# First retention rows loaded in the order of their use, and split queries stacked with their gap in one transfer

## The reference, cut to what matters

```python
h = s4d_kernel(log_dt, inv_A_real, A_imag, B, C=x, L=512)      # (16, 192, 512)
h = h + retention(layernorm(h))                                # 8 heads, keys 64, values 128
h = h + top1_attention(layernorm(h))                           # 16 heads of 32

# retention, per batch of 192 tokens
q, k = rope(x @ Wq), rope(x @ Wk);  v, g = x @ Wv, x @ Wg
scores = (q * 64 ** -0.5) @ k.T * decay_mask
o = rmsnorm(scores @ v) * g_norm_weight * (g * sigmoid(g))
out = o @ Wo
# top-1 attention: every key and value is that of the head which the gate picks for the token
gating = softmax(x @ W_gate.T);  indicator = one_hot(argmax(gating))
k_shared = sum_h(indicator * k);  v_shared = sum_h(indicator * max(gating) * v)
y = softmax(causal(q @ k_shared.T / sqrt(32))) @ v_shared
```

## Time and profile before

| what | us |
|---|---|
| median of three runs | 1326.13 (1326.09 to 1329.57) |
| the profiled execution, its own time | 1326.51 |
| its span, first to last instruction | 1323.5 |
| PE busy | 1223.8 |
| DVE, ACT, POOL busy | 723.7, 559.0, 519.9 |
| DMA moved | 150.60 MB, mean 114 GB/s |

### The profile page before, as it was taken

How to read it: one execution, slowest core, us unless ns; L and a number is a source line. 1 busy time by engine, 2 the same in 40 slices (tenths; PEclk the granted TensorE clock), 3 DMA queues, 4 the chain that set the end, 5 groups by cost and what they waited for, 6 DMA issues and landing times. The chain is left out here.

```text
span 1323.5 us, 23061 instructions
## 1 busy us (share of the span) xinstructions
PE 1223.8 (92%) x8280; PEld 1014.5 (77%) x8280; DVE 723.7 (55%) x1360; ACT 559.0 (42%) x1769; POOL 519.9 (39%) x722
## 2 busy tenths in 40 slices
PE   0389999999999999589999999989999999999997
PEld 0378888888888887467878887768888788887875
DVE  7686655566576532354554446434465555645444
ACT  3344333444443322334443332224555555454546
POOL 2757766766676631233332333120321213122121
PEclk9999999999999999799999999998999999999999
DMA  4132223222222226965665545141232515234041
GB/s 154 68 117 96 112 96 120 88 104 104 111 104 101 99 91 233 274 176 173 205 184 177 155 139 144 48 104 40 74 80 66 126 29 136 70 77 107 17 118 33
DMA packets 81792, 150.60 MB, mean 114 GB/s; under 512 B 11664, under 2 KB 44560, under 8 KB 80144
## 3 DMA queue, kind: packets, MB, share of 16 engines
q1 hardware_dynamic: 81680, 149.15, 36.4%
HBM read 67.19 MB, written 56.62 MB: 94 GB/s over the span
## 5 line engine op out<-in xcount | busy, mean ns | idle before, releaser
L1670 ACT ACTIVATE probs<-psum,row_max 128x128 f32<-128x128 f32 (+1 forms) x384 | 142.9, 388 | 51.1 <-DVE row_max L1836 39.3
L1002 ACT ACTIVATE square_scratch<-psum 128x128 f32<-128x128 f32 x192 | 50.7, 274 | 177.4 <-PE psum L1235 177.4
L1836 DVE TENSOR_REDUCE row_max<-psum 128x2 f32<-128x384 f32 (+1 forms) x128 | 79.2, 619 | 83.9 <-PE psum L2066 43.6
L1966 POOL TENSOR_TENSOR h_rows<-h_rows,y_normed 128x512 f32<-128x512 f32 x24 | 30.7, 1280 | 227.9 <-DVE y_normed L1853 227.9
L1943 POOL TENSOR_TENSOR picked_rows<-picked_rows 128x768 f32<-128x768 f32 (+1 forms) x64 | 61.1, 954 | 103.0 <-DVE picked_rows L1818 99.3
L1175 POOL TENSOR_TENSOR rr<-ss,consts_r 128x3 f32<-128x3 f32 x64 | 15.0, 234 | 202.3 <-ACT square_scratch L1002 198.0
L710 PE MATMUL psum<-m,basis 128*128 128x64 f32 x384 | 48.8, 284 | 43.7 <-POOL basis L662 43.7
L681 POOL TENSOR_TENSOR stage<-stage 128x512 f32<-128x512 f32 x48 | 81.6, 1718 | 14.5 <-DVE stage L563 14.5
L1844 DVE COPY raw_f<-psum 128x512 f32<-128x512 f32 x64 | 44.2, 691 | 78.3 <-PE psum L2079 78.2
L710 PEld LDWEIGHTS psum<-m,basis 128*128 128x128 f32 x384 | 49.7, 203 | 45.4 <-issue 43.7
L1670 ACT ACTIVATION_READ_ACCUMULATOR probs<-psum,row_max 128x1 f32 x384 | 80.5, 210 | 0.0
(11 more groups left out here) (269 smaller groups left out, 3603.9 us busy)
## 6 DMA issues: line engine op xcount, KB each, us to landing
qk<-stage SPq DMA_DIRECT2D x24, 512.0 KB, 2.7
v<-stage SPq DMA_DIRECT2D x24, 512.0 KB, 2.6
g<-gate_rows SPq DMA_DIRECT2D x24, 512.0 KB, 2.7
qk_rows<-qk SPq DMA_DIRECT2D x16, 512.0 KB, 7.0
stage<-in_w_r SPq DMA_DIRECT2D x6, 1024.0 KB, 5.1
h_tok<-h_rows SPq DMA_DIRECT2D x24, 256.0 KB, 2.0
q_stack_even<-q_t_high SPq DMA_DIRECT2D x64, 96.0 KB, 2.2
q_stack_even<-q_t_low SPq DMA_DIRECT2D x64, 96.0 KB, 2.2
```

Source lines behind the costliest of these rows:

```text
L1002: last = nc.scalar.activation(sqs[:, h % 2, t], psum[:, OB[h % 2], t * RV:(t + 1) * RV], ACT.Square, accum_out=ss[:, h % 2, t:t + 1])
L1670: last = nc.scalar.activation(pr[:, g % 2, c], psum[:, SB[g % 3], c], ACT.Exp, bias=mx[:, g % 3, x:x + 1], accum_out=dsum[:, t, h:h + 1])
L1836: V.reduce_max(mx[:, g % 3, 0:nh], psum[:, SB[g % 3], 0:nh * w].rearrange("p (h n) -> p h n", h=nh), AX, negate=True).then_inc(s_max.sem, 1)
L1966: G.tensor_tensor(h, h, yn[:, (NT * i + t) % 2].rearrange("p h f -> p (h f)"), ALU.add).then_inc(added.sem, 1)
```

## The change

Two things are changed. **First**, the order in which SP fetches what stage Q needs first, and where the output weights are made ready. `prefetch` keeps q/k tiles 0 and 1, the constants and v tiles 0 and 1. A new `prefetch_more`, ahead of the last unit's gate store, waits for the q/k store and loads q/k tile 2, waits for the v store and loads v tile 2, and loads gate tiles 0 and 1. Then come q/k tiles 0 and 1 of pair 1, gate tile 2, q/k tile 2 of pair 1, and last the output weights. ScalarE makes the high parts after squares 3 and 5 of pair 0, and VectorE the low parts at m = 2 and 3, not 1 and 2.

**Second**, `q_t_high` and `q_t_low` take the row layout of the stack, 192, 64 zeros, 192 for each chunk, with the zeros written once in them and not in the stacks. One DMA then moves a whole row of 448 for 4 heads, so a pair's stack takes 16 DMAs. SP waits for the zeros before the first, PE no longer does. `picked_rows` and `probs` move up, `y_heads_t` lies elsewhere, and VectorE waits for the last h2 stores before it writes the second half of `picked_rows`.

```diff
--- before.py
+++ after.py
@@ -284,6 +284,8 @@ stage_p sync
         def slot(u):
+            if step_of(u, -1) == (0, NU - 1):
+                prefetch_more(sp)
             if valid(step_of(u, -1)):
                 sp.wait_ge(gated.sem, gated.of(step_of(u, -1), 2))
@@ -907,12 +909,19 @@ stage_q prefetch
         units["filtered"](sp)
         for t in range(2):
             load_qk(sp, 0, t)
-            load_v(sp, 0, t)
-            load_g(sp, 0, t)
         sp.dma_start(cr[:, :], d["consts_r"]).then_inc(const_in, 16)
         sp.dma_start(gnorm_t[:, 0:1], d["g_norm"]).then_inc(const_in, 16)
-        for n in range(NW):
-            sp.dma_start(raw[:, n], d["w_f"][n].rearrange("p k f -> p (k f)")).then_inc(w_in[n], 16)
+        for t in range(2):
+            load_v(sp, 0, t)
+
+    def prefetch_more(sp):
+
+        units["qk_stored"](sp)
+        load_qk(sp, 0, 2)
+        units["v_stored"](sp)
+        load_v(sp, 0, 2)
+        for t in range(2):
+            load_g(sp, 0, t)
@@ -965,15 +974,14 @@ stage_q sync
-        units["qk_stored"](sp)
-        load_qk(sp, 0, 2)
-        units["v_stored"](sp)
-        load_v(sp, 0, 2)
+        for t in range(2):
+            load_qk(sp, 1, t)
         units["g_stored"](sp)
         load_g(sp, 0, 2)
         units["h_stored"](sp)
-        for t in range(NT):
-            load_qk(sp, 1, t)
+        load_qk(sp, 1, 2)
+        for n in range(NW):
+            sp.dma_start(raw[:, n], d["w_f"][n].rearrange("p k f -> p (k f)")).then_inc(w_in[n], 16)
         pairs(slot)
@@ -1025,8 +1033,6 @@ stage_q scalar
             if i == 0:
                 act.wait_ge(const_in, 32)
-                w_copy(0)
-                w_copy(1)
@@ -1042,6 +1048,8 @@ stage_q scalar, in the loop over t
                 o_squares(i, 2 * t + 1)
+                if i == 0:
+                    w_copy(t - 1)
                 if ahead:
                     qkt_evac(i + 1, t, 1)
@@ -1132,8 +1140,8 @@ stage_q vector, in the loop over m
                 if back:
                     add_h(i - 1, m - 1)
-                elif m < HG - 1:
-                    split_weights(m - 1)
+                elif m > 1:
+                    split_weights(m - 2)
@@ -1385,12 +1393,13 @@ stage_f, buffers
-    qhi = sb("q_t_high", [P, KC, TP], F32R)
-    qlo = sb("q_t_low", [P, KC, TP], F32R)
+    q_high_rows = sb("q_t_high", [P, KC * QW + R], F32R)
+    q_low_rows = sb("q_t_low", [P, KC * QW + R], F32R)
+    qhi, qlo = [[m[:, c * QW:c * QW + 4 * P].rearrange("p (b n) -> p b n", b=2)[:, :, 0:T] for c in range(KC)]
+                for m in (q_high_rows, q_low_rows)]
     sel = sb("picked_rows", [P, 2, NT, FH, FD])
     pr = sb("probs", [P, 2, 512])
-    yT = sb("y_heads_t", [P, FH // HB, P])
-    sb("gap_f", [P, 512])
+    sb("gap_f", [P, 384])
@@ -1414,7 +1423,8 @@
-    sb("gap_y", [P, 2048])
+    yT = sb("y_heads_t", [P, FH // HB, P])
+    sb("gap_y", [P, 1536])
@@ -1459,7 +1469,7 @@
-    q_stacked = Signal(sem("q_stacked"), 1, 32 * 16)
+    q_stacked = Signal(sem("q_stacked"), 1, 16 * 16)
@@ -1569,13 +1579,14 @@ stage_f sync, q_stack
+            if i == 0:
+                sp.wait_ge(half_ready, 3)
             for s in range(4):
-                src = (qhi, qhi, qlo, qlo)[s]
+                src = (q_high_rows, q_high_rows, q_low_rows, q_low_rows)[s]
                 for h in range(4):
-                    for b in range(2):
-                        sp.dma_start(qsT[i % 2][s * FD:(s + 1) * FD, h:FH:4, b * 2 * P:b * 2 * P + T].bitcast(F32),
-                                     src[h * FD:(h + 1) * FD, :, b * T:(b + 1) * T].bitcast(F32)
-                                     ).then_inc(q_stacked.sem, 16)
+                    sp.dma_start(qsT[i % 2][s * FD:(s + 1) * FD, h:FH:4].bitcast(F32),
+                                 src[h * FD:(h + 1) * FD, 0:KC * QW].rearrange("p (c n) -> p c n", c=KC).bitcast(F32)
+                                 ).then_inc(q_stacked.sem, 16)
@@ -1648,7 +1659,8 @@ stage_f scalar, q_split
-            nc.scalar.activation(qhi[:, c], psum[:, q_bank(i, c), 0:TP], ACT.Copy, scale=SCALE_F).then_inc(q_high.sem, 1)
+            nc.scalar.activation(qhi[c], psum[:, q_bank(i, c), 0:TP].rearrange("p (b n) -> p b n", b=2), ACT.Copy,
+                                 scale=SCALE_F).then_inc(q_high.sem, 1)
@@ -1903,6 +1915,7 @@ stage_f vector, run
                 pick(0, 0, t)
+            ended["stored"](dve)
             pick(0, 1, 0)
@@ -1969,8 +1982,9 @@ stage_f gpsimd, run
-            for q in qsT:
-                G.memset(q[:, :, T:2 * P].bitcast(F32), 0.0).then_inc(half_ready, 1)
+            for q in (q_high_rows, q_low_rows):
+                G.memset(q[:, 0:KC * QW].rearrange("p (c n) -> p c n", c=KC)[:, :, T:2 * P].bitcast(F32), 0.0
+                         ).then_inc(half_ready, 1)
@@ -2046,7 +2060,6 @@ stage_f tensor, scores
             if n == 0:
-                pe.wait_ge(half_ready, 3)
                 pe.wait_ge(kt_out.sem, kt_out.at(i, 1))
```

More of the change, by code:

```diff
@@ L252, in slots, with sync @@
             slot((0, n))
-    def sync(sp, prefetch):
+    def sync(sp, prefetch, prefetch_more):
         for s in (*c_in, *h_store, qk_store, v_store, g_store):
@@ L1370, in stage_q @@
     }
-    return Stage(sync, scalar, vector, gpsimd, tensor), prefetch, ended
+    return Stage(sync, scalar, vector, gpsimd, tensor), prefetch, prefetch_more, ended
 def stage_f(nc, sem, sb, psum, ident, d, ended):
@@ L1808, in q_split @@
             dve.wait_ge(q_high.sem, q_high.at(i, c + 1))
-            V.scalar_tensor_tensor(qlo[:, c], psum[:, q_bank(i, c), 0:TP], SCALE_F, qhi[:, c].bitcast(F32), ALU.mult,
-                                   ALU.subtract).then_inc(q_low.sem, 1)
+            V.scalar_tensor_tensor(qlo[c], psum[:, q_bank(i, c), 0:TP].rearrange("p (b n) -> p b n", b=2), SCALE_F,
+                                   qhi[c].bitcast(F32), ALU.mult, ALU.subtract).then_inc(q_low.sem, 1)
         def pick(i, x, t):
@@ L2254, in program @@
         with ExitStack() as s:
-            retention, prefetch, ended = stage_q(nc, sem, scope(s), psum, ident, d, last_unit)
+            retention, prefetch, prefetch_more, ended = stage_q(nc, sem, scope(s), psum, ident, d, last_unit)
         with ExitStack() as s:
@@ L2260, in _ @@
             def _(sp):
-                units.sync(sp, prefetch)
+                units.sync(sp, prefetch, prefetch_more)
                 f = attention.sync(sp)
```

## The result

The changed kernel takes **1318.4 us** (median; 1316.7 to 1319.9) beside 1327.2 for the kernel before in the same job: a ratio of 0.9928, 95% interval 0.9912 to 0.9944. It is faster by some 9 us, where 17.9 were forecast, and the time lies 2.4 us above the range. The profiled execution took 1319.74, its span 1318.0. That is near the upper end of its runs, and before's profiled span of 1323.5 was a short one (the time outside the span was 3.0 in that execution, about 2 in nearly all other runs of before). Its mean granted clock was 0.980 as well, where most runs of before have 0.975 to 0.977. Over 1326 us that is some 10 us more at half clock (an estimate from these means), and no profile shows where. So the two profiles show 5.5 us of span where the medians show 9: they serve to place the gains, not to weigh them to the microsecond, and some 3 us of the gain are placed by no trace.

What follows compares the result with a forecast made beforehand. TensorE, busy for 92% of the span, was taken to bound the kernel, so only its waits and clock could pay. Hand-over 10.5 plus query stack 7.4 gave 17.9 us: median 1308.3 from 1326.13, range 1303 to 1316.

Steps and rivals of the forecast that it cites:

- the landing of pair 1's rows: Hand-over: q/k tile 0 of pair 1 lands at 534.8, PE waits 0.8 us, `values` start at 535.9, not 544.78.
- the stack's rate: Query stack: 3.67 MB at 232 GB/s takes 15.8 us; PE starts at 886.6, not 892.04, gaining 5.4 us.
- the clock behind the stack: After the stack, half clock costs 4.9 us; 2.0 of it was to be won back.
- Tile 2 at the hand-over: Pair 0's tile 2, read back from DRAM, lands near 528, before PE wants it at 530.7: the wait goes whole.
- 1.5 of start: Load of tile 2 into 64 partitions: about 1.5 us of start, an estimate, before 2.1 us for 0.5 MB.
- The splits: VectorE's weight splits in pair 0: 2.3 us gained at m = 1, some 1.5 of 2.34 lost at m = 3.
- The sum for the border: First border, the hand-over with pair 0's weight work: 9.7 + 2.3 - 1.5 = 10.5 us gained, bounds 7 and 12.
- the slower rival: Output weights land last in the queue and delay the squares of head 4; 1332 us if at 570; chance 0.04.
- The choice between bytes and issuing: Query stack: bytes bind, landing at 886.5; the rival, bound by issuing, lands at 881.7 and gives 1307 us, chance 0.08.
- data late: Rival at the hand-over: pair 1's q/k or gate 2 comes 2 to 4 us later; 1312 us, chance 0.20.
- the clock stays down: Rival: slow stretch repeats in full, or later logits run slow more often; 2 to 4 us back, 1311, chance 0.14.
- both lower bounds (7 and 3): Least gains: 7 us at the hand-over (pair 1's q/k and gate 2 late), 3 at the stack (start 889, slow stretch stays).

Runs made afterwards that it cites:

- rows_alone: Changed kernel with q/k tile 0 of pair 1 issued ahead of v tile 2 and all gate tiles: 1318.1 us, ratio 0.9931 to the kernel before.
- rows_first: Changed kernel with q/k tile 0 of pair 1 loaded ahead of gate tiles 0 and 1, tile 1 behind all gates: 1316.4 us, ratio 0.9911.
- stack_alternate: Changed kernel with the stack's 16 transfers issued to partition groups in order 0, 2, 1, 3: 1316.1 us, ratio 0.9923.
- stack_wide: Changed kernel with each stack moved by 4 transfers of 128 partitions, not 16 of 32, same bytes, heads not regrouped: 1311.7 us, ratio 0.9873.
- tile2_wide: Changed kernel with every third tile loaded by two transfers of 128 partitions and half the columns, not 64 and all, fetching other rows: 1320.0 us, ratio 0.9931.
- split_early: Changed kernel with VectorE's two weight splits back at m = 1 and 2, ScalarE's copies left late: 1321.5 us, ratio 0.9959.

## Why the prediction was wrong

The direction and the two places were right; the size was half. Three steps of the sum failed: the landing of pair 1's rows, the stack's rate, and the clock behind the stack. Along the trace:

**Tile 2 at the hand-over: right.** Store to landing 4.8 us (about 3 forecast), load issued at 524.19 (523.2), no wait, first scores at 532.71 (532.9), full clock up to there. The "1.5 of start" in that step has no row behind it; the load landed 3.9 us after its issue, where the sum had 3.6. The 5.3 MB ahead of the old store are 5.5 by the transfers' sizes, which nothing in the sum uses.

**Pair 1's rows: the first term that failed.** "It lands at 534.8" took 2.6 MB (2.1 ahead and 0.5 of rows) from 527 on, served in order of issue at about 400 GB/s. The rows came at 537.1, and up to there the full engines had moved 3.2 MB at 316 GB/s:

```profile
527.00:537.10 10.10, 4.68 (x38) 3.61 (x37) 2.35 (x5) 3.85 (x7) 0.00 (x0) 1.00 1.00 316
```

The rate was too high (the 410 was a row of another mixture, with the output weights in it), and some 0.6 MB of later transfers shared the engines, as they do in `rows_alone`. PE idled 3.3 us, not 0.8, and its clock fell to half again, so the 0.8 us that the first `values` were to save by the clock weren't saved. Together 3.3 us of the first gating (543.41, forecast 540.15). In all seven profiles with this code the idling was 2.75 us or more, so the step failed in each of them.

**The splits: one size right, one wrong.** m = 1 gave 2.27 (2.3 forecast). m = 3 took 2.36, not 1.5, with PE at half clock ahead of it (558.4 to 565.2). In `rows_first` and `stack_alternate` the same stretch, from the third mask wait to the first output matmul, was 1.39 us longer than before's, near the 1.5; the split and the clock aren't told apart here. The sum for the border was 6.5 in place of 10.5: 3.3 less by the rows, 0.9 less here, and 0.1 more at m = 2. The ScalarE copies were covered (ScalarE idles 4.07 us behind the second), and ScalarE waits for no weights; the slower rival has no support.

**The stack's rate: wrong.** The 232 GB/s was scaled up from a stretch that was busy for 0.66, and a share scaled up is not a rate measured. It is 209 at full share; PE's wait was 3.9, not 1.1, and the gain on the wait 2.6, not 5.4. The choice between bytes and issuing was right, and the 218 of the Trainium skill's "SBUF — State Buffer", Door 1, was nearer than my number. `stack_wide` shows the cause.

**The clock: the sign was wrong.** I took 2.0 us back of 4.9. In fact 1.3 were lost: the slow stretch was as long as before and lay over more work, since PE stood idle for less of it (0.9 us for 3.8). The error in this term, 3.3 us, is a little more than that in the wait itself. In the three profiles with 10.2 us at half clock the time to the first `values` was 19.1, for before's 19.0: there nothing was lost, and in none of the eight was anything won back. The stretch from 898 on shows PEclk 1.00; 886 to 896 shows 0.50.

Sum at stage F's first `values`: 17.9 less 4.0 (hand-over), 0.6 (a slow stretch more in stage Q, near 828), 2.8 (stack) and 3.3 (clock) is 7.2, as read. **The rivals** "data late" and "the clock stays down" both happened, each near its price. I had priced them as if only one could: 1312 or 1311. Together they reach 1314.7, and the stack's longer wait, which no rival held, makes most of the rest. The two aren't independent, since both grow with PE's idling. The range's end, 1316, was the sum of both lower bounds (7 and 3), and both terms came in below: 6.5 and 1.3 along the trace. The hand-over's bound allowed for late rows but not for a dearer split as well; the stack's allowed for a start at 889 and a slow stretch that stays, but not for one that covers more work than before.

Two smaller things. The base, 1326.1, was the median of three runs; over all jobs before's median lay at 1327.2 to 1328.3. So some 1 us of the 10.1 between forecast and result is the base's, and 9 are the gain's. And what remains open: why full engines move only 217 to 307 GB/s at the hand-over. The partitions' span explains a little of it (`tile2_wide`); stores and read-backs running side by side would be a reason, but no run separates them. Why pair 1's rows take 6.7 to 10.4 us in kernels that are the same up to there is open too.

**The better kernel** is the change with the logits ahead of the first scores: 1311.1 us, 1.2% below before and some 0.5% below the change. It takes one moved line.

## What to carry to other kernels

Let "late data" and "low clock" happen together when you price a shortened wait: an idling that was cut from 6.5 to about 4 us gave back nothing of the clock in eight profiles, one filled with work gave back 3.2 to 4.4 us, so look for independent work for the rest of the wait before counting the clock. Take the rate of a transfer from a stretch with full share, the same number of partitions and the same mixture of loads and stores, and don't treat a queue as served in order. When a chain of loads must all land before the work goes on, reordering can move the wait without removing it, as it did here. Take several profiles of one kernel before you read a gain of a microsecond or two from a single one.

## What the runs showed of the hardware

- **Transfers within SBUF over 32 partitions moved at little over half the rate.** 209 and 213 GB/s at full share, in either order of quadrants; 367 to 383 with 128 partitions (and transfers four times as large). The busy share was near 1 in both, so it doesn't tell the rate.
- **A load shares the engines with what is issued behind it**: 6.6 us for 512 KB with one store of 512 KB ahead, while at least 0.65 MB of later loads passed.
- **A GpSimd operation that met VectorE's split ended with it.** On three columns it takes 0.20 us elsewhere, but 2.25 while the split runs:

```profile
565.33 2.25 POOL L1184 TENSOR_TENSOR rr<-rr,small_q 128x3 f32<-128x3 f32 x1
```

and VectorE's split over the same time:

```profile
565.19 2.34 DVE L1119 SCALAR_TENSOR_TENSOR wo_low<-wo_raw,g_norm,wo_high 128x2048 fp32r<-128x2048 f32 x1
```

The two end within 0.1 us of each other. The same happens at 556.26 (1.78 us beside the split at 555.64), and twice in the kernel before (1.78 and 1.93 us). In `split_early`, where no GpSimd operation fell beside a split, none took over 1 us. That it wasn't on PE's path here is my reading of the order of the chain, and no run tests it.
